# First stage, routing, the context's norm, the second attention's opening and the last experts' norm, rewritten together

## The reference

```
x = x + cross_attention_0(layernorm(x), ctx, mask)      # 16 heads of 8
x = x + experts_0(layernorm(x))                          # 32 experts of 64, groups of 4, top 6, and shared ones
x = x + cross_attention_1(ctx, latents = layernorm(x))   # 16 heads of 64, keys: 256 context + 256 latent rows
x = x + experts_1(layernorm(x))                          # 8 experts of 512, top 1, with a capacity
```

## Time and profile before

| | |
|---|---|
| runs | 1246.11, 1247.11, 1247.45 us; median 1247.11 |
| the profiled execution | 1248.01 us, its span 1246.2 |
| mean granted clock of TensorE | 0.908 |
| busy, share of the span | TensorE 76%, VectorE 73%, ScalarE 63%, GpSimd 46% |
| A: q's last low part done, first row scores | 45.5, 54.53 |
| C: stage's first instruction, second pair's first product | 253.2, 311.6 |
| E: stage's first product, first exponential | 475.2, 533.93 |
| F: stage's first instruction, last of the parts | 1083.3, 1119.9 |

### The profile page before, as it was taken

One profiled execution on the slowest core, in us unless ns is written; L12 is line 12 of the kernel. 1 busy time (PEld: TensorE's weight loads), 2 busy tenths in 40 slices (PEclk: granted clock), 3 DMA queues, 4 the chain that ended last, 5 costly groups with the idle time before them and its releaser, 6 DMA issues. The chain is left out here.

```text
span 1246.2 us, 25731 instructions
## 1 busy us (share of the span) xinstructions
PE 945.9 (76%) x9389; PEld 611.7 (49%) x9394; DVE 915.4 (73%) x1924; ACT 790.5 (63%) x1496; POOL 579.2 (46%) x514
## 2 busy tenths in 40 slices
PE   3478888752999975488888889898888879438646
PEld 2145555521444431256665656566666657424345
DVE  7579989767566674478788888878788887359931
ACT  3157777839455545189898898989898887341022
POOL 2100000020677865367677676757677673220325
PEclk8689999965999996689999999999999999769978
DMA  6302110040000000111111011111111110220140
GB/s 244 74 2 28 15 21 6 2 146 1 19 19 25 19 1 1 26 27 28 27 27 23 16 26 23 23 27 27 27 28 27 19 27 10 112 120 1 41 134 26
DMA packets 73838, 46.59 MB, mean 37 GB/s; under 512 B 55056, under 2 KB 70911, under 8 KB 72646
## 3 DMA queue, kind: packets, MB, share of 16 engines
q1 hardware_dynamic: 72296, 42.40, 14.1%
q0 software_dynamic: 1440, 2.82, 0.7%
HBM read 26.52 MB, written 8.77 MB: 28 GB/s over the span
## 5 line engine op out<-in xcount | busy, mean ns | idle before, releaser
L1489 POOL TENSOR_TENSOR e_p_lo<-e_probs,e_p_hi 128x1024 f16<-128x1024 f32 x64 | 136.4, 2131 | 127.2 <-ACT e_probs L1782 127.2
L1837 DVE TENSOR_REDUCE e_neg_max<-e_row_scores 128x1 f32<-128x512 f32 x256 | 169.4, 682 | 12.3 <-PE e_row_scores L1561 10.6
L1780 ACT ACTIVATE e_p_hi<-e_scores 128x512 f16<-128x512 f32 x256 | 153.3, 599 | 34.0 <-PE e_scores L1665 32.1
L1664 PE MATMUL e_scores<-e_q_stack,e_k_stack 128*128 128x256 f16 x512 | 125.1, 274 | 6.0 <-DVE e_p_lo L1842 5.6
L1472 POOL TENSOR_TENSOR e_raw<-e_raw,e_inv 128x512 f32<-128x512 f32 x96 | 98.9, 1044 | 65.1 <-DVE e_inv L1822 65.1
L1665 PE MATMUL e_scores<-e_q_high,e_k_high 128*128 128x256 f16 x512 | 125.0, 274 | 0.0
L1484 POOL TENSOR_TENSOR e_natural<-e_raw,e_natural 128x512 f16<-128x512 f32 x96 | 109.2, 1157 | 9.5 <-ACT e_natural L1711 9.5
L767 POOL TENSOR_TENSOR c_h_lo<-c_hidden,c_h_hi 128x512 f16<-128x512 f32 x68 | 78.9, 1160 | 68.1 <-ACT c_h_hi L944 66.2
L1577 PE MATMUL e_mix<-e_v_cols,e_p_hi 128*128 128x65 f16 x1024 | 107.2, 192 | 4.4 <-POOL e_p_lo L1489 3.3
L1578 PE MATMUL e_mix<-e_v_cols,e_p_hi 128*128 128x64 f16 x1024 | 107.3, 195 | 0.0
L1579 PE MATMUL e_mix<-e_v_cols,e_p_lo 128*128 128x65 f16 x1024 | 106.8, 191 | 0.0
(11 more groups left out here) (384 smaller groups left out, 2841.5 us busy)
## 6 DMA issues: line engine op xcount, KB each, us to landing
e_k_high<-e_k_stack SPq DMA_DIRECT2D x64, 128.0 KB, 2.7
e_q_high<-e_q_stack SPq DMA_DIRECT2D x32, 128.0 KB, 2.6
w<-in_w SPq DMA_DIRECT2D x2, 2048.0 KB, 9.9
c_w<-in_w SPq DMA_DIRECT2D x17, 192.0 KB, 2.4
placed_scratch<-in_no_rows SPq DMA_DIRECT2D x1, 2313.0 KB, 16.1
a_mask_q<-in_mask_q SPq DMA_DIRECT2D x1, 2048.0 KB, 10.2
a_mask_k<-in_mask_k SPq DMA_DIRECT2D x1, 2048.0 KB, 14.6
parts_scratch<-a_parts SPq DMA_DIRECT2D x2, 1024.0 KB, 4.0
```

What stands on the lines that cost most here:

```text
L1489: nc.gpsimd.tensor_tensor(p_lo[buf][i][:], probs[i][:], p_hi[buf][i][:], ALU.subtract).then_inc(lo_done[i], 1)
L1664: pe.matmul(out, k_stack[hf][:, h, cols], q_stack[hf][:, h, :], start=(kt % 2 == 0), stop=False, skip_group_check=True)
L1780: act.activation(p_hi[p % 2][i][:, at, :], scores[n % SBANKS][:], ACT.Exp).then_inc(exp_done, 1)
L1837: dve.tensor_reduce(neg_max[buf][:, 2 * i + qt:2 * i + qt + 1], row_scores[qt % RBANKS][:], AX.X, ALU.max, negate=True).then_inc(max_done, 1)
```

## The change

It makes five edits in one.

Stage A: x and mask_q come in four DMAs each; the norm uses `statistics` and `normed` on VectorE instead of sums and squares; the mask bias (now 0 or 1, scaled by a new identity `ident_m` in the matmul) is made tile by tile, with a sum of masked keys beside it that replaces the mask's reduction; the jobs are k, t0, t1, q0, t2, q1, t3, q2, q3, v in eight banks; k and q are stored in four DMAs each and loaded as soon as the half that they need is there; the q stacks are cleared by GpSimd; the row of ones or zeros is loaded once per stack, so that a batch has seven DMAs instead of eight.

```diff
-        jobs = [("k", g) for g in range(4)] + [("v", g) for g in range(4)]
-        jobs += [(kind, g) for g in range(4) for kind in ("t", "q")]
+        jobs = [("k", g) for g in range(4)] + [("t", 0)]
+        for g in range(4):
+            jobs += [("t", g + 1)] * (g < 3) + [("q", g)]
+        jobs += [("v", g) for g in range(4)]
...
+            for g in range(4):
+                rows(g)
+            mask(0)
...
+            for g in range(4):
+                store("k", g)
+            sp.wait_ge(zeroed, 2 * RING)
+            for b in range(RING):
+                load("k", b)
+            store("q", 0)
+            store("q", 1)
+            load("q", 0)
+            load("q", 1)
+            store("q", 2)
+            load("q", 2)
+            store("q", 3)
...
+            def norm(g):
+                at = slice(4 * g, 4 * g + 4)
+                dve.wait_ge(mask_in[g > 0], 48 if g else 16)
+                for t in tiles_of(g):
+                    ins = dve.tensor_scalar(bias_q[:, t, :], mask_q[:, t, :], 0.0, None, ALU.is_equal, ALU.add, accum_out=masked[:, t:t + 1])
+                chain.then(ins)
+                chain.then(dve.scalar_tensor_tensor(seen[:, at], masked[:, at], float(S), inv[:, at], ALU.is_lt, ALU.mult))
+                normed(dve, nrm, xr, moments, seen, tiles_of(g)).then_inc(norm_done, 1)
```

```diff
                 chain.then(ins)
+                chain.then(dve.memset(top[:, :, count:8], NOWHERE))
                 for t in range(NT):
-                    ins = dve.max_index(top_at[:, t, :], top[:, t, :], values[:, t, :])
+                    ins = dve.match_replace(out[:, t, :], top[:, t, :], values[:, t, :], GONE)
                 chain.then(ins)
-                chain.then(dve.tensor_copy(top_atf[:], top_at[:]))
...
-                chain.then(dve.tensor_tensor(hit, numbers, places, ALU.is_equal))
-                chain.then(dve.tensor_reduce(out[:].rearrange("p t e -> p (t e)"),
...
+            chain.then(dve.scalar_tensor_tensor(whole, picked_g[:].unsqueeze(3).to_broadcast((P, NT, G0, per)), GONE, whole,
+                                                ALU.is_equal, ALU.mult))
```

Second attention's opening: VectorE waits for the cleared tiles only at the first value; unit 0's `norm` and `low` are VectorE's (L1472 and L1484 in form), and the list is new:

```diff
+    for j in range(6):
+        out += [("norm", j, 0), ("hi", j, 0)]
         if j:
-            out.append(("d", KQ[j - 1] + (1,)))
...
+            out.append(("low", j - 1, 0))
+        if j > 1:
+            out.append(turns[j - 2])
+    one = [(name, t, 1) for name, t in KQ]
+    out += [turns[4], ("low", 5, 0), one[0], turns[5], ("d", one[0])]
+    for job in one[1:4]:
+        out += [job, ("d", job)]
+    rows = [("r", i, qt, 0) for i in range(2) for qt in range(QT)]
+    out += rows[:2] + [one[4]] + rows[2:] + [("d", one[4]), ("m", 0), one[5], ("d", one[5])]
+    values = [("v", t, 0) for t in range(KT)]
+    rows = [("r", i, qt, 1) for i in range(2) for qt in range(QT)]
+    out += rows[:1] + [("root", 1)] + rows[1:2] + [values[0], ("d", values[0])] + rows[2:3] + [values[1], ("d", values[1])] + rows[3:]
+    out += [values[2], ("d", values[2]), values[3], ("d", values[3])]
```

Last experts: the norm is by groups with `statistics`, `centre` and `norm` as in C; VectorE's memsets (L2239 to L2242) move behind the four low parts. ScalarE:

```diff
-            layer_norm_all_act(act, centred, squared, var_done, root_done, nrm, squares, small, 2)
+            root(0)
+            root(1)
+            root(2)
+            take(0)
+            take(1)
+            root(3)
+            take(2)
+            take(3)
...
             act.copy(carried[:, :, 2 * D], ids[:]).then_inc(carried_done, 1)
-            act.copy(w1_hi[:, 1:E1], w1[:, 1:E1]).then_inc(w_hi_done, 1)
...
-                if n == FB:
+                if n == 0:
                     act.wait_ge(shifted, 1)
                     act.activation(logits[:], logits[:], ACT.Exp).then_inc(powers, 1)
...
                 relu(0, n, fb, c % 2, 512)
+                if n == FB - 1:
+                    act.copy(w1_hi[:, 1:E1], w1[:, 1:E1]).then_inc(w_hi_done, 1)
```

More of the change, by code:

```diff
@@ new lines, in project_layer0 @@
+        mask_q, mask_k = sb("mask_q", [P, NT, S], I32), sb("mask_k", [P, NT, S], I32)
+        ctx_t = sb("ctx_t", [P, T], F32)
+        w3 = sb("w3", [P, 3, D], F32)
+        w3_hi, w3_lo = sb("w3_hi", [P, 3, D], F16), sb("w3_lo", [P, 3, D], F16)
+        ctx_hi, ctx_lo = sb("ctx_hi", [P, T], F16), sb("ctx_lo", [P, T], F16)
+        x_hi, x_lo = sb("x_hi", [P, T], F16), sb("x_lo", [P, T], F16)
+        parts = sb("parts", [P, 4, T], F16)
+        banks = [ctx.enter_context(nc.psum_tensor(f"a_bank{i}", [P, 512], F32)) for i in range(8)]
@@ L169, in lows @@
         def lows(n):
-            return sum(1 for m in split if m <= n)
+            return sum(1 for kind, _ in jobs[:n + 1] if kind != "v")
         block = ctx.enter_context(nc.Block())
@@ L454, in step @@
                 if ahead:
-                    pe.wait_ge(loaded[after], 16 * 2 * STACK_DMAS * (turn + (buf + 1) // RING + 1))
+                    pe.wait_ge(loaded[after], 16 * STACK_DMAS * (turn + (buf + 1) // RING + 1))
                 for p in range(NP0):
@@ L984, in _, with weight_high @@
                     act.activation(out[:, cols], ring[g % 3][:], ACT.Identity, bias=norm_w[:, 1:2], scale=norm_w[:, 0:1]).then_inc(ctx_taken, 1)
+            pieces = [(wq_hi, wq, 512 * n) for n in range(2)] + [(wkv_hi, wkv, 512 * n) for n in range(4)]
+            def weight_high(n):
+                hi, whole, at = pieces[n]
+                act.copy(hi[:, at:at + 512], whole[:, at:at + 512]).then_inc(ctx_steps, 1)
             def more_silus(k, first=False):
@@ L995, in more_silus @@
                         high(k - 1, NCH - 1)
+                    if isinstance(k, int):
+                        for n in range(NCH * (k - 1) + c, min(NCH * (k - 1) + c + 1, 6)):
+                            weight_high(n)
             more_silus(1, first=True)
-            with act.Fori(2, PAIRS + 1) as k:
+            more_silus(2)
+            with act.Fori(3, PAIRS + 1) as k:
                 more_silus(k)
@@ L1086, in _, with pick @@
                                          choice[:].rearrange("p t (g e) -> p (t g) e", g=G0), AX.X, ALU.max))
-            def pick(values, n, count, out):
+            def pick(values, count, out):
                 for t in range(NT):
@@ L1884, in _ @@
                     invert(event[1])
+                elif name == "norm" and event[2] == 0:
+                    first_norm(event[1])
+                elif name == "low" and event[2] == 0:
+                    first_low(event[1])
                 elif name in ("tk", "tq") and TURNED_BY == "V":
```

420 lines of the change are left out of this document (219 added, 201 removed).

## The result

The changed kernel took 1218.2 us (median of 4, 1216.5 to 1218.9) against 1246.99 for the kernel before: -28.8 us, ratio 0.9768 with a 95% interval of 0.9751 to 0.9785. The forecast was 1211.5, with 1202 to 1220. Boundaries are the stages' first instructions. The gain is 0.81 of the one forecast.

A forecast was written before the change was run, and what follows sets the result against it. TensorE fills the steady loops, while chains of waits set the time in the openings that the change edits. -15.0 - 14.0 - 7.3 + 0.7 = -35.6 gave 1211.5 us against the median; range 1202 to 1220.

The forecast's parts named there:

- A: First stage, up to the first row scores: these start at 39.5 instead of 54.53, -15.0 us (bounds -18 and -11).
- F: Last experts, norm by groups: the parts, held by GpSimd's w1_lo, end at 1120.6, +0.7 us (bounds -6.3 and +1.0).
- Rival 1: In the last experts, the parts slip through ahead of GpSimd's hold: -42.6 in all, 1204.5 us; chance 0.20.
- rival 4: Edits miss the path: DMA queue limits A, C's opening still gives 10 and E 7: 1229 us; chance 0.05.
- C: First experts stage: routing -10.3, weight pieces -2.3 and tail -1.4, together -14.0 us.
- The picks: In C's routing, with match_replace at 0.16: the first pick 1.6 us shorter, the second 6.9.
- The parts leading TensorE's line: In C's routing: the second pair's parts no longer wait 3.3 us behind TensorE's last context transposes.
- Loop and tail: In C: GpSimd's weight pieces one to a pair, -2.3; qk_gain leaves and turn_back(0) goes ahead, -1.4.
- E: Second attention's opening: first exponential at 526.6 instead of 533.93, -7.3 us (bounds -6 and -9.5).
- B: First attention, from the first row scores to C's first statistics: forecast 0.
- Rival 2: Openings overlap worse: memset hold in A, dear match_replace, slow clock in E: -26, 1221 us; chance 0.19.
- Rival 3: TensorE stays at 1.2 GHz in C's routed loop: 1265 us with 25 slow chunks; chance 0.02.

The follow-up runs named there:

- experiment 2: The changed kernel with GpSimd's low part of w1 made to wait until VectorE's parts are done in the last stage: 1214.4 us, ratio 0.9717.
- experiment 3: The changed kernel with GpSimd's low part of w1 cut into seven pieces of one expert each, without waits between: 1219.9 us, ratio 0.9751.
- Experiment 1: The changed kernel with the K loads of batches 1 and 2 moved behind the q stores in SyncE's first-stage list: 1218.9 us, ratio 0.9746.
- experiment 6: The changed kernel with the old picks put back (max_index, copy, compare, sum): 1225.8 us, ratio 0.9809.
- experiment 5: The changed kernel itself measured again, as a control: 1218.9 us, ratio 0.9758.
- Experiment 7: The changed kernel with the second attention's old function and opening order put back: 1228.8 us, ratio 0.9843.
- experiment 8: The changed kernel with the edits of Experiment 1, experiment 2 and experiment 4, and GpSimd's last two stack memsets held back: 1207.5 us, ratio 0.9661.
- experiment 4: The changed kernel with the first four context squares moved from ahead of the sigmoid to behind the silus: 1220.5 us, ratio 0.9777.

## Why the forecast was right, and where not

**F, the wait that takes the place of the one removed.** Right as to the mechanism, shown by experiments 2 and 3. Two terms were off. The parts' first wait was taken to end at once with the exponential moved ahead; there it meets a table load of 1.28 us. The trace before had it too, behind the last relu and right ahead of the exponential, and so on the path already; the forecast moved the exponential without it. From the timeline of the kernel before, ScalarE:

```profile
1110.38 0.69 ACT L2198 ACTIVATE f_hidden<-f_hid,b 128x512 f32<-128x512 f32 x1 [0.32 <-PE f_hid L2079]
1111.09 1.28 ACT L2206 ACT_TABLE_LOAD   x1
1112.38 0.31 ACT L2206 ACTIVATE f_logits<-f_logits 128x128 f32<-128x128 f32 x1
```

VectorE went on 4.7 us earlier instead of 6.3. The relus and the copy of w1_hi follow the exponential on ScalarE, so the load put them off too: GpSimd started 30.2 us into the stage, not 29.2, and the hold ended later: +2.0 to the last part instead of +0.7. Rival 1, that the parts slip through, fell.

**A, -11.0 for -15.0.** Two terms failed. The first: "The block ends with that, not with a DMA: the stores and loads of the earlier parts are issued by 35". SyncE's last store was issued at 42.4: the store of q's first quarter took 8.4 us to land in the queue behind nine K loads, and SyncE could not go on before. This is what rival 4 asked about, and for some 2.7 us it was right (43.54, less the 0.8 of the block's change and the 40.0 of `bias_k`). Experiment 1 shows the queue, but gives back only 1.3 of it. The second: the hold by GpSimd's memsets had no place in the sum; it stood as a bound, at most one memset of 1.76 in each of two groups, at the normalising instructions. It came at the small instruction ahead of them, where the layout has it end near 9.7 (4.4, 5.1 of statistics and its own 0.17) and it ended at 13.16. That is the whole 3.5 us by which q's last low part was late (37.8 for 34.3). In that execution x came 1.0 later than taken and the hold itself was 2.3; but in all eight profiles with these memsets the instruction ended at 13.15 to 13.17, wherever it had started, so an earlier x would not have helped. The v products, priced at the low clock, were 2.3 cheaper than taken, and this hid a part: the engines ended at 40.0, only 1.3 later than the 38.7 of the forecast and not 3.5. That is luck.

**C, -11.3 for -14.0.** The picks were right within 0.3 (-1.5 and -6.9), with the match at the price of the row it was nearest to, 0.14 and 0.16 for 0.16; experiment 6 confirms the sum. The parts leading TensorE's line was right (-3.0 for -3.3). "The chain reaches the group maximum 1.7 later than before" was 2.8 in this profile, but 1.9 to 2.0 in the six others with the same code, so most of that miss is TensorE's clock in one execution (0.61 against 0.77 to 0.80) and not the layout. Loop and tail gave 2.4 of 3.7 (3.0 in experiment 5): the 1.49 us wait is gone and VectorE's chunks, from the second on, are 2.00 to 2.32 apart in a steady pattern, 2.16 on average, but TensorE reached the full clock 5.1 us behind the pair's first product instead of 3.0. In experiment 5 the whole stage gave -12.7.

**E, -8.8 for -7.3.** The layout held: sums done 8.9 us in (8.6 forecast), root at 12.9 (12.7) with its first instruction held to the end of GpSimd's additions, first exponential at 50.2 (51.4). Experiment 7 shows that the gain lasts.

The result lies in the range that was given, but not between the 1207 and 1217 of the forecast itself. A, C and F together came out 8.2 us dearer than forecast; E's 1.5 and B's 1.3, which is chance, took 2.8 of that back. Rival 2, that the openings overlap worse, was nearer than the forecast: its 1221 lay 2.8 us above the result, the forecast 6.7 below. It was near for other reasons than its own: of its three causes the hold by the memsets came, inside its bound of 3.5, the dear match did not, and the slow clock came in C and not in E. What it lacked was the queue. Rival 4's own parts (10, 7 and F's 0.7) make 1231, not 1229. Rival 3, TensorE's clock in the routed loop, did not come, but a small form of it did, ahead of the loop and at its first chunks.

## What to carry over

When an opening is laid out again, give the DMA queue a line of its own beside the engines': a store on the path is as late as what was issued ahead of it, and loads that nobody needs yet belong behind it. Give each long GpSimd instruction a line too, and ask which short VectorE instruction runs beside it; a wait that puts the GpSimd work behind the short ones (experiment 2) took a 7 us hold away, and cutting it up did not. An activation's table load belongs in the sum with it when it is moved; three idle activations, placed where ScalarE waited anyway, took 1.28 us and a little more off the path at each of three places. Last, compare several profiles of the same code before a difference is put down to an edit: one profile of each made the moved squares look worth 1.9 us at the second pair, and experiment 8 found nothing.

## What had not been expected of the hardware

- VectorE's instruction started at 10.73 was held for 2.43 us, longer than one memset of GpSimd (5.29 for three, 1.76 each, so one ended near 11.4) and until the last one ended at 13.13. In the seven other profiles with these memsets it started between 9.96 (experiment 4, 3.21 us long) and 11.72 (experiment 5, 1.43) and ended at 13.15 to 13.17 each time, past one boundary in five of them. In experiment 3 each held instruction got in at a piece's end. What tells the two apart was not tried. The statistics instructions ran beside the same memsets at their usual 0.87 for four.
- The Trainium skill ("ScalarE: Activation LUTs", "What ACT_TABLE_LOAD costs") states 1283 ns for a table load and another 1380 ns to drain for each switch. The loads here lasted 1.28, and taking one off the path gave 1.28 at two places and 1.45 at the third: no run here shows the drain. In the kernel before (the rows under F above) the load starts 0.02 us behind the end of the last relu, and the exponential 0.01 behind the load.
- Profiles of unchanged code differ by 4 us in the first attention (196.7 to 200.7) and by 8 in the last stage's end (120.4 to 128.4, experiment 3 the longest, there at a granted clock of 0.82, 0.85 in the first profile). What sets this was not tried.
